# Causal attention in two score passes: first unit's stacked rows in sequence, value products in halves, and an earlier copy of the output's first half

## The chip, the cores and the metric

The kernel runs on one core of a Trainium2 chip. The metric is device time in microseconds: the time of one launch, in several runs, with their median. One further execution was profiled; every row below is of that one.

The engines have short names here, as in the profile: PE is TensorE's matmul side and PEld its weight loads, DVE is VectorE, ACT is ScalarE, POOL is GpSimd, SP is SyncE. SP and ACT each issue DMAs on a hardware queue of their own: q1 in the profile is SP's, q10 is ACT's.

## The reference, cut to what matters

The input is x with 2 sequences of 1024 tokens and 128 features. Four stages add to it one after the other: a causal attention at three sets of weights ("a"), six layers of local attention with a feed-forward part, a causal attention with linear biases ("b"), and the six layers again. The change touches the two causal stages only. What they compute, per sequence and set of weights, with 16 heads of 8 features:

```python
q, k, v = proj(Wq, bq), proj(Wk, bk), proj(Wv, bv)          # 16 heads, 8 features each
scores = einsum('bhqd,bhkd->bhqk', q, k) * scale            # causal: k <= q
m = max(scores, axis=-1)
e = exp(scores - m)
w = e / (sum(e, axis=-1) + 1e-06)
out = einsum('bhqk,bhkd->bhqd', w, v)
```

Stage "a" has six such units (two sequences by three weight sets), with an output projection and two layer norms behind them; stage "b" has two units with a bias per head and no norm.

## The kernel before, in words

All of a causal stage is in the function `causal` (from line 266). Each engine runs its own program, written out by hand, and all of them walk the same order: an outer loop over steps g (`STEPS`), an inner loop over 38 items n. Semaphores tie them together.

**Steps and items.** A unit's 16 heads are four quads of four heads; step g works on quad g % 4 of unit g // 4. Two score passes run at once. The first pass, of quad g, takes the scores with queries on partitions, item by item as in `FIRST` (38 items, each one bank of 512 columns, some of one matmul, some of two or four, eight of them on the diagonal with a mask matmul ahead); DVE reduces each item to its maxima (line 674). The second pass, of quad g - 2, takes the scores with keys on partitions and the negated maxima as three further rows of the contraction (`SECOND`, 36 items, eight with a mask); ACT takes the exponential of each (line 772). Stage "a" has 24 quads, "b" has 8. So a stage has two steps with the first pass alone, 22 or 6 with both, and two with the second alone, which are its tail.

**Stacked rows.** q and k are split into three bf16 parts, written to a scratch in DRAM (line 488, SP), and read back so that 48 partitions hold the six products of parts that are needed: lower heads on partitions 0 to 63, upper heads on 64 to 127. A set is six DMAs of 8 partitions by 16 KB. For the first unit of a stage SP issues q's rows, the lower in step -4 and the upper in step -2 (`stack`, line 504), and ACT issues k's rows, lower and then upper, in `stack_first_keys` (line 818) at step -3. For later units SP issues both. The lower rows are needed by quads 0 and 1 of a unit, the upper by quads 2 and 3: at line 545 PE waits, in steps 0 and 2 of a unit, for `stack_in[0]` or `stack_in[1]`. The two passes of one step lie on different halves of the partitions, so that they run side by side in PE.

**Banks.** The first pass has PSUM banks 0 to 2, the second 3 to 5, in turn. Before the scores of an item PE waits until the item three before it has been reduced (`s1_free`) or exponentiated (`s2_free`). Bank 6 holds the output of a quad, first half (512 queries), then second half. Bank 7 is for side matmuls (`beside`): projections, transposes, layer norms, one at most every third item, behind items with n % 3 == 1.

**Value products.** `GROUPS` cuts the 36 items of the second pass into ten groups of four or two items. When the last item of the group after it has been issued (n = 7, 9, 13, 17, 21, 25, 29, 33, 35, and 2 of the next step for the last), PE issues all value matmuls of a group in one go (`values`, line 579; matmuls at line 594): pieces of 128 to 512 columns, each from 128 keys to 32 output partitions, so that four heads run side by side on PE's columns. The first group has 16 pieces, the second 8, the third 4, the fourth 16, the next four 4 each, then 8 and 4. They are f32 and show as two records each. Exponentials lie in `pt`, which has room for three groups.

**Copies of the output.** The first half of a quad's output is complete after three groups, the second after ten. ACT copies each out of bank 6 (`take_out`, line 782): the first half behind the exponential of item 16, the second behind item 5 of the next step. Before the fourth group, at item 17, PE waits for the first copy (`ot_done`), and before the first group of the next quad, at item 7, for the second.

Of the kernel before, what the change touches and what calls it, by code (L numbers as in the profile page):

```python
# [86 lines left out]

FIRST = first_items()
SECOND, GROUPS = second_items()
GROUP_OF = [k for k, (lo, hi) in enumerate(GROUPS) for _ in range(lo, hi)]  # L90
PLAN = (("causal", "a"), ("layers", 0), ("causal", "b"), ("layers", 1))


def build(nc, t, out, scratch):
    with ExitStack() as ctx:
# [149 lines left out]
        at = [0]  # L245
# [20 lines left out]
        def causal(kind):  # L266
# [62 lines left out]
            with ExitStack() as local:  # L329
# [133 lines left out]
                with nc.Block() as block:  # L463
                    @block.sync
                    def _(sp):
                        def place_maxima(g):
                            if not 0 <= g < 4 * U:
                                return
                            G = 4 * u0 + g
                            rows, h0, par = rows_of(g, KS)  # L470
                            sp.wait_ge(m_step, 4 * G + 4)
                            if G:
                                sp.wait_ge(m_in, 48 * G)
                            for c in range(3):
                                r = rows.start + KF + c
                                sp.dma_start(qs[par][r:r + 1, h0:h0 + 4, :].rearrange("p h (q n) -> p (h q) n", n=P),
                                             mparts[0:4 * QT, c, :]).then_inc(m_in, 16)

                        def write_parts(u):
                            if not 0 <= u < U:  # L480
                                return
                            I = u0 + u
                            if I >= 2:
                                for h in range(2):
                                    sp.wait_ge(stack_in[h], 192 * (I - 1))
                            for a in range(2):
                                sp.wait_ge(split[3], 4 * I + 2 + 2 * a)
                                sp.dma_start(scratch[u % 2, a].rearrange("c p n -> p c n"), parts[:, a, :, :]).then_inc(part_out[a], 16)

                        def stack(u, h):  # L490
                            if not 0 <= u < U:
                                return
                            I = u0 + u
                            if u >= 2:
                                sp.wait_ge(s2_ready, 36 * (4 * (I - 2) + 2 * h + 2))
                            if I:
                                sp.wait_ge(stack_in[h], 192 * I)
                            for a, (combo, to) in enumerate(((COMBO_Q, qs[u % 2]), (COMBO_K, ks[u % 2]))):
                                if u == 0 and a == 1:
                                    continue  # L500
                                sp.wait_ge(part_out[a], 16 * (I + 1))
                                for n, c in enumerate(combo):
                                    r = 64 * h + 8 * n
                                    sp.dma_start(to[r:r + 8, :, :],
                                                 scratch[u % 2, a, c, 64 * h:64 * h + 64].rearrange("(h d) n -> d h n", d=HD)).then_inc(stack_in[h], 16)

                        def next_weights(u):
                            if not 2 <= u < U:
                                return
                            sp.wait_ge(side_free, order["value", u - 2, 1] + 1)  # L510
                            load_unit(sp, u)

                        def next_out_weights(u):
                            if not 1 <= u < U or kind == "b":
                                return
                            sp.wait_ge(side_free, order["join", u - 1, 1] + 1)
                            load_out(sp, u)

                        for g in STEPS:
                            i, q = divmod(g, 4)  # L520
                            place_maxima(g - 1)
                            if q == 0:
                                write_parts(i + 1)
                                stack(i + 1, 0)
                            elif q == 1:
                                next_out_weights(i - 1)
                            elif q == 2:
                                next_weights(i + 2)
                                stack(i + 1, 1)

                    @block.tensor
                    def _(pe):
# [43 lines left out]
                                    if x == len(second) - 1:  # L576
                                        ins.then_inc(s2_ready, 1)

                        def values(g, k):
                            if not 0 <= g < 4 * U:  # L580
                                return
                            G = 4 * u0 + g
                            c = 0 if k < 3 else 1
                            if k == 0:
                                pe.wait_ge(vq_ready, G + 1)
                                if G:
                                    pe.wait_ge(ot_done, 2 * G)
                            elif k == 3:
                                pe.wait_ge(ot_done, 2 * G + 1)
                            lo, hi = GROUPS[k]  # L590
                            pe.wait_ge(s2_free, len(SECOND) * G + hi)
                            pieces = [(b, piece) for b in range(lo, hi) for piece in SECOND[b]]
                            for b, (j, kt, q0, w, diag, at) in sorted(pieces, key=lambda one: (one[1][1], one[1][0])):
                                ins = nc.tensor.matmul(ps[32 * j:32 * j + 32, 6, q0 - c * CH:q0 - c * CH + w], vq[:, G % 2, kt, j, :],
                                                       pt[:, (len(GROUPS) * G + k) % 3, b - lo, at:at + w],
                                                       start=diag and kt % 4 == 0, stop=True, skip_group_check=True)
                            ins.then_inc(values_done, 1)

                        def beside(what, u, x):

# [50 lines left out]
                        for g in STEPS:  # L651
                            for n in range(len(FIRST)):
                                scores(g, n)
                                if n == 2:
                                    values(g - 3, len(GROUPS) - 1)
                                for k in range(len(GROUPS) - 1):
                                    if n == GROUPS[k + 1][1] - 1:
                                        values(g - 2, k)
                                if n % 3 == 1 and n < 36 and side_at(g, n // 3):
                                    beside(*side_at(g, n // 3))  # L660

# [100 lines left out]
                    def _(act):  # L762
# [48 lines left out]
                        def stack_first_keys():  # L811
                            act.wait_ge(part_out[1], 16 * (u0 + 1))
                            for h in range(2):
                                if u0:
                                    act.wait_ge(stack_in[h], 192 * u0)
                                for n, c in enumerate(COMBO_K):
                                    r = 64 * h + 8 * n
                                    act.dma_start(ks[0][r:r + 8, :, :],
                                                  scratch[0, 1, c, 64 * h:64 * h + 64].rearrange("(h d) n -> d h n", d=HD)).then_inc(stack_in[h], 16)

                        for g in STEPS:
                            if g == -3:
                                stack_first_keys()
                            for n in range(len(FIRST)):
                                if n < len(SECOND):
                                    exponentials(g - 2, n)
                                if n == 5:
                                    take_out(g - 3, 1)
                                elif n == 16:
                                    take_out(g - 2, 0)  # L830
                                if n % 3 == 2 and n < 37:
                                    before = side_at(g, n // 3 - 1) if n >= 3 else None
                                    if before and before[0] == "project":
                                        part(*before[1:], 1)
                                    if side_at(g, n // 3):
                                        beside(*side_at(g, n // 3))
# [957 lines left out]
```

## Time and profile before

| | |
|---|---|
| median of 3 runs | 5032.56 us (5029.35 to 5033.88) |
| the profiled execution's own time | 5031.75 us |
| its span, first to last instruction | 5030.0 us |
| PE busy | 4547.3 us, 90% |
| PEld busy | 2702.9 us, 54% |
| DVE busy | 3756.1 us, 75% |
| ACT busy | 3470.0 us, 69% |
| mean granted clock of TensorE | 0.940 |
| line 674, DVE's reductions of the first pass, stage "a" | 912 of 657 ns, 561.8 us |
| line 772, ACT's exponentials, stage "a" | 864 of 600 ns, 475.3 us |

The span is what lies between the first and the last instruction; the rest of the time is launch and end. Busy shares are means over four stages with different limits: here the first causal stage takes about the first fifth of the span, the second lies between 2844 and 3204 us, and the rest is the layers, which the change does not touch. A granted clock of 1.0 is 2.4 GHz, of 0.5 it is 1.2 GHz. A matmul's recorded end is modelled, so starts are safer to read than lengths: matmuls of one kind overlap in the records.

### The profile page before, as it was taken

What the parts mean: (1) busy time and instruction counts of PE and PEld (TensorE: products, weight loads), DVE (VectorE), ACT (ScalarE), POOL (GpSimd) and SP (SyncE); (2) the same over time, 40 slices, a digit from 0 to 9 for tenths busy, and PEclk for the clock granted to TensorE, in tenths of its full rate; (3) what the DMA queues carried; (4) which work ended last, traced back from release to release, by engine and by line L of the source; (5) the groups of instructions that cost most, each with busy time, mean ns of one, the idle gap of its engine ahead of it and who ended that gap; (6) DMA issues with size and microseconds to landing.
All of it is one profiled execution on the core that took longest, in us unless ns stands there. A gap on an engine that the chain in (4) does not pass through costs nothing. (4 is left out here: it accounts for less than half of the span.)

```text
span 5030.0 us, 122883 instructions
## 1 busy us (share of the span) xinstructions
PE 4547.3 (90%) x49788; PEld 2702.9 (54%) x49788; DVE 3756.1 (75%) x5802; ACT 3470.0 (69%) x5475; POOL 2201.6 (44%) x1271
## 2 busy tenths in 40 slices
PE   5998989869999999999999599789999999999997
PEld 2333433336666666666666233256666666666664
DVE  4777777257888888888887277278888888888884
ACT  1666666437878887887877136368888787888884
POOL 1111010036656565665654010066566565656561
PEclk6999999779999999999999679789999999999998
DMA  3211220000000000000000120000000000000000
GB/s 80 42 38 28 37 41 3 2 32 10 10 6 19 2 24 2 15 10 15 10 6 2 43 46 2 32 10 10 2 15 10 15 10 15 10 2 24 2 6 9
DMA packets 70035, 87.77 MB, mean 17 GB/s; under 512 B 22532, under 2 KB 44288, under 8 KB 68864
## 3 DMA queue, kind: packets, MB, share of 16 engines
q1 hardware_dynamic: 67720, 76.41, 6.5%
q8 instruction: 416, 6.82, 0.6%
q10 hardware_dynamic: 1728, 3.15, 0.4%
q14 instruction: 171, 1.40, 0.1%
HBM read 65.11 MB, written 13.63 MB: 16 GB/s over the span
## 5 line engine op out<-in xcount | busy, mean ns | idle before, releaser
L1078 PE MATMUL ps<-l_wqk,l_xa 128*128 128x512 f32 x1536 | 772.7, 627 | 42.8 <-DVE l_rs L1544 42.8
L674 DVE TENSOR_REDUCE a_pm<-ps 128x1 f32<-128x512 f32 (+3 forms) x912 | 561.8, 657 | 213.1 <-PE ps L568 208.1
L1188 PE MATMUL ps<-l_yb,l_mh 128*128 128x256 f32 x3072 | 710.1, 381 | 2.5 <-issue 2.5
L772 ACT ACTIVATE a_pt<-ps 128x512 f32<-128x512 f32 x864 | 475.3, 600 | 334.1 <-PE ps L574 331.9
L1501 POOL TENSOR_TENSOR l_pn<-l_pe,l_rl 128x1024 f32<-128x1024 f32 x192 | 365.2, 1902 | 558.6 <-DVE l_rl L1582 558.5
L1188 PEld LDWEIGHTS ps<-l_yb,l_mh 128*128 128x128 f32 x3072 | 564.3, 190 | 74.7 <-issue 5.6
L1544 DVE TENSOR_TENSOR l_rs<-ps,l_tab 128x512 f32<-128x512 f32 x768 | 491.1, 681 | 0.0
L1078 PEld LDWEIGHTS ps<-l_wqk,l_xa 128*128 128x128 f32 x1536 | 276.4, 194 | 379.4 <-issue 298.4
L1492 POOL TENSOR_TENSOR l_qkn<-l_rc,l_rn 128x1024 f32<-128x1024 f32 x192 | 386.4, 2013 | 202.5 <-DVE l_rn L1562 202.5
L1484 POOL TENSOR_TENSOR l_rc<-l_rc,l_rs 128x1024 f32<-128x1024 f32 x192 | 452.0, 2354 | 44.3 <-DVE l_rs L1544 44.3
L1552 DVE TENSOR_REDUCE l_ss<-l_sq 128x16 f32<-128x1024 f32 x384 | 464.9, 1211 | 2.8
L1172 PE MATMUL ps<-l_ptl,l_xw 64*128 64x256 f32 x3072 | 444.2, 407 | 19.6 <-DVE l_yb L1592 13.4
L1331 ACT ACTIVATE l_sq<-ps 128x1024 f32<-128x1024 f32 x384 | 388.9, 1013 | 89.0 <-PE ps L1078 87.5
L1254 PE MATMUL ps<-l_lnx,l_w 128*128 128x512 f32 (+1 forms) x576 | 319.1, 637 | 113.7 <-ACT l_gl L1444 101.0
L1402 ACT ACTIVATE l_yb<-ps 128x256 f32<-128x256 f32 x768 | 251.2, 380 | 220.9 <-PE ps L1172 220.7
L1172 PEld LDWEIGHTS ps<-l_ptl,l_xw 64*128 64x128 f32 x3072 | 270.0, 188 | 240.8 <-issue 136.0
L1484 POOL TENSOR_TENSOR lnc<-lnc,l_rs 128x1024 f32<-128x1024 f32 x96 | 226.0, 2354 | 335.2 <-DVE l_rs L1544 335.2
L568 PE MATMUL ps<-a_ks,a_qs 48*128 48x128 bf16 (+3 forms) x1728 | 319.2, 290 | 58.4 <-DMA a_ks<-scratch 38.4
L1592 DVE COPY l_yb<-ps 128x256 f32<-128x256 f32 x768 | 288.2, 417 | 60.7 <-PE ps L1172 40.7
L1484 POOL TENSOR_TENSOR lnq<-lnq,l_rs 128x1024 f32<-128x1024 f32 x96 | 226.3, 2357 | 240.0 <-DVE l_rs L1544 240.0
L1366 ACT ACTIVATE l_kt<-ps 128x512 f32<-128x512 f32 x384 | 207.8, 594 | 177.9 <-PE ps L1084 177.9
L574 PE MATMUL ps<-a_qs,a_ks 51*128 51x128 bf16 (+3 forms) x1728 | 307.9, 286 | 0.9 <-ACT a_pt L772 0.7
(225 smaller groups left out, 9054.3 us busy)
## 6 DMA issues: line engine op xcount, KB each, us to landing
l_wqk<-in_lWqkv SPq DMA_DIRECT2D x24, 512.0 KB, 4.5
scratch<-a_parts SPq DMA_DIRECT2D x12, 768.0 KB, 4.2
a_qs<-scratch SPq DMA_DIRECT2D x72, 128.0 KB
a_ks<-scratch SPq DMA_DIRECT2D x60, 128.0 KB
l_wvt<-in_lWvT SPq DMA_DIRECT2D x12, 512.0 KB, 4.9
l_wo<-in_lWo SPq DMA_DIRECT2D x12, 512.0 KB, 6.6
l_w<-in_lW SPq DMA_DIRECT2D x12, 341.0 KB, 2.8
scratch<-b_parts SPq DMA_DIRECT2D x4, 768.0 KB, 4.7
```

The lines of the kernel that those rows point to most:

```text
L568: ins = nc.tensor.matmul(ps[:, bank1, at1:at1 + w], qs[par][rows, h0 + j, qt * P:(qt + 1) * P], ks[par][rows, h0 + j, k0:k0 + w], start=no ...
L674: nc.vector.tensor_reduce(to, src, AX.X, ALU.max).then_inc(s1_free, 1)
L772: nc.scalar.activation(pt[:, K % 3, n - GROUPS[k][0], :], ps[:, 3 + N2 % 3, :], ACT.Exp).then_inc(s2_free, 1)
L1078: last = nc.tensor.matmul(ps[:, x, :], xa[:, u, o:o + P], wqk[:, a * INNER + x * CH:a * INNER + (x + 1) * CH], start=True, stop=True)
L1172: last = nc.tensor.matmul(ps[:, 4 + e, w * 256:(w + 1) * 256], xw[rows, t % 2, ww, :], ptl[rows, :, 32 * ww:32 * ww + 32], start=w == 0, s ...
L1188: last = nc.tensor.matmul(ps[:, 6, 0:2 * P], mh[:, h, :], yb[:, n % 2, h, :], start=h == 0, stop=h == LH - 1, skip_group_check=True)
L1331: nc.scalar.activation(sq[:, a, :].rearrange("p (x n) -> p x n", x=2), ps[:, 0:2, :], ACT.Square).then_inc(N["qk"[a] + "_squared"], 1)
L1484: nc.gpsimd.tensor_tensor(turned(t, a), turned(t, a), rs[:, a, :], ALU.add).then_inc(N["qk"[a] + "_rotated"], 1)
L1492: nc.gpsimd.tensor_tensor(qkn[:, a, :].rearrange("p (h d) -> p h d", d=LD), turned(t, a).rearrange("p (h d) -> p h d", d=LD), rn[:, a, :]. ...
L1501: nc.gpsimd.tensor_tensor(pn[:, :, :], pe_[:, :, :], rl[:].unsqueeze(2).to_broadcast([P, LH, 2 * WIN]), ALU.mult).then_inc(N["p_done"], 1)
L1544: ins = nc.vector.tensor_tensor(dsin[:, :, lo:lo + 32], src[:, :, hi:hi + 32], tab[:, 2 * a + 1, t % QT, lo:lo + 32].unsqueeze(1).to_broad ...
L1552: nc.vector.tensor_reduce(ss[:, a, :], sq[:, a, :].rearrange("p (h d) -> p h d", d=LD), AX.X, ALU.add).then_inc(N["qk"[a] + "_summed"], 1)
```

## The change

Three edits, in the functions of the causal stages. First, for the first unit of a stage the upper stacked rows are issued only when the lower ones, of q and of k, have landed: SP waits for `stack_in[0]` in `stack`, ACT in `stack_first_keys`. Second, a group's value matmuls are issued in two halves: the first where the whole group was, the second one item later (for the last group at items 1 and 2 in place of 2). Groups of more than four pieces are cut by pieces; groups of four pieces have each piece cut in two by columns, which makes eight. Third, ACT copies the first half of the output behind item 14 in place of 16.

```diff
--- before.py
+++ after.py
@@ -87,6 +87,21 @@
 
 FIRST = first_items()
 SECOND, GROUPS = second_items()
+
+
+def half_groups():
+
+    out = []
+    for lo, hi in GROUPS:
+        pieces = sorted(((b, piece) for b in range(lo, hi) for piece in SECOND[b]), key=lambda one: (one[1][1], one[1][0]))
+        if len(pieces) > 4:
+            out.append((pieces[:len(pieces) // 2], pieces[len(pieces) // 2:]))
+        else:
+            out.append(tuple([(b, (j, kt, q0 + h * w // 2, w // 2, diag, at + h * w // 2)) for b, (j, kt, q0, w, diag, at) in pieces] for h in range(2)))
+    return out
+
+
+HALVES = half_groups()
 GROUP_OF = [k for k, (lo, hi) in enumerate(GROUPS) for _ in range(lo, hi)]
 PLAN = (("causal", "a"), ("layers", 0), ("causal", "b"), ("layers", 1))
 
@@ -495,6 +510,8 @@
                                 sp.wait_ge(s2_ready, 36 * (4 * (I - 2) + 2 * h + 2))
                             if I:
                                 sp.wait_ge(stack_in[h], 192 * I)
+                            if u == 0 and h == 1:
+                                sp.wait_ge(stack_in[0], 192 * (u0 + 1))
                             for a, (combo, to) in enumerate(((COMBO_Q, qs[u % 2]), (COMBO_K, ks[u % 2]))):
                                 if u == 0 and a == 1:
                                     continue
@@ -576,25 +593,25 @@
                                     if x == len(second) - 1:
                                         ins.then_inc(s2_ready, 1)
 
-                        def values(g, k):
+                        def values(g, k, part):
                             if not 0 <= g < 4 * U:
                                 return
                             G = 4 * u0 + g
                             c = 0 if k < 3 else 1
-                            if k == 0:
+                            if part == 0 and k == 0:
                                 pe.wait_ge(vq_ready, G + 1)
                                 if G:
                                     pe.wait_ge(ot_done, 2 * G)
-                            elif k == 3:
+                            elif part == 0 and k == 3:
                                 pe.wait_ge(ot_done, 2 * G + 1)
                             lo, hi = GROUPS[k]
                             pe.wait_ge(s2_free, len(SECOND) * G + hi)
-                            pieces = [(b, piece) for b in range(lo, hi) for piece in SECOND[b]]
-                            for b, (j, kt, q0, w, diag, at) in sorted(pieces, key=lambda one: (one[1][1], one[1][0])):
+                            for b, (j, kt, q0, w, diag, at) in HALVES[k][part]:
                                 ins = nc.tensor.matmul(ps[32 * j:32 * j + 32, 6, q0 - c * CH:q0 - c * CH + w], vq[:, G % 2, kt, j, :],
                                                        pt[:, (len(GROUPS) * G + k) % 3, b - lo, at:at + w],
                                                        start=diag and kt % 4 == 0, stop=True, skip_group_check=True)
-                            ins.then_inc(values_done, 1)
+                            if part == 1:
+                                ins.then_inc(values_done, 1)
 
                         def beside(what, u, x):
 
@@ -651,11 +668,11 @@
                         for g in STEPS:
                             for n in range(len(FIRST)):
                                 scores(g, n)
-                                if n == 2:
-                                    values(g - 3, len(GROUPS) - 1)
+                                if n in (1, 2):
+                                    values(g - 3, len(GROUPS) - 1, n - 1)
                                 for k in range(len(GROUPS) - 1):
-                                    if n == GROUPS[k + 1][1] - 1:
-                                        values(g - 2, k)
+                                    if n in (GROUPS[k + 1][1] - 1, GROUPS[k + 1][1]):
+                                        values(g - 2, k, n - GROUPS[k + 1][1] + 1)
                                 if n % 3 == 1 and n < 36 and side_at(g, n // 3):
                                     beside(*side_at(g, n // 3))
 
@@ -813,6 +830,8 @@
                             for h in range(2):
                                 if u0:
                                     act.wait_ge(stack_in[h], 192 * u0)
+                                if h:
+                                    act.wait_ge(stack_in[0], 192 * (u0 + 1))
                                 for n, c in enumerate(COMBO_K):
                                     r = 64 * h + 8 * n
                                     act.dma_start(ks[0][r:r + 8, :, :],
@@ -826,7 +845,7 @@
                                     exponentials(g - 2, n)
                                 if n == 5:
                                     take_out(g - 3, 1)
-                                elif n == 16:
+                                elif n == 14:
                                     take_out(g - 2, 0)
                                 if n % 3 == 2 and n < 37:
                                     before = side_at(g, n // 3 - 1) if n >= 3 else None
```

## Rows read from the trace of the kernel before

**Rows 1.** Windows by stage, first causal stage: start, steady part, tail.

```profile
core 0: us, PE busy (x) PEld busy (x) DVE busy (x) ACT busy (x) POOL busy (x), PEclk, DMA share, GB/s
26.00:70.70 44.70, 3.80 (x7) 0.89 (x6) 3.00 (x4) 4.70 (x8) 9.09 (x8) 0.60 0.42 92
...
276.00:884.00 608.00, 549.32 (x5557) 236.21 (x5553) 468.22 (x869) 383.90 (x699) 57.10 (x109) 0.96 0.15 29
...
909.00:981.20 72.20, 68.05 (x456) 21.99 (x454) 1.91 (x4) 40.05 (x77) 1.73 (x5) 0.65 0.02 3
```

**Rows 2.** Timelines of SP, ACT, PE at both stages' starts: start, length, [idle <- releaser].

```profile
40.47 5.20 SPq L504 DMA_DIRECT2D a_qs<-scratch  x12
...
89.05 8.49 SPq L488 DMA_DIRECT2D scratch<-a_parts  x2
...
44.92 12.79 ACTq L818 DMA_DIRECT2D a_ks<-scratch  x12
81.29 0.63 ACT L791 ACTIVATE a_parts<-a_qkf 128x512 bf16<-128x512 f32 x1 [42.50 <-DVE a_qkf L705]
...
70.75 1.46 PE L568 MATMUL ps<-a_ks,a_qs 48*128 48x512 bf16 x3 [38.40 <-DMA a_ks<-scratch]
...
2894.14 1.46 PE L568 MATMUL ps<-b_ks,b_qs 54*128 54x512 bf16 x3 [35.26 <-DMA b_ks<-scratch]
```

**Rows 3.** DMA queues (packets, MB, share) in 45:53, 54.5:68.5 (both), 71:77 us.

```profile
q1 hardware_dynamic: 314, 0.57, 52.9%
...
q10 hardware_dynamic: 408, 0.75, 27.3%
q1 hardware_dynamic: 396, 0.72, 25.8%
...
q10 hardware_dynamic: 258, 0.48, 52.4%
```

**Rows 4.** Waits from 131 to 981 us: total us, times, longest.

```profile
DVE a_pm L674 <- PE ps L568: 159.3, 228, 3.4
PEld ps L568 <- DVE a_pm L674: 133.3, 234, 2.0
...
PEld ps L594 <- issue: 61.4, 218, 1.7
...
PEld ps L594 <- ACT a_ot L782: 25.6, 24, 4.3
```

**Rows 5.** Waits from 2955 to 3204 us (second causal stage).

```profile
PEld ps L594 <- ACT b_ot L782: 9.3, 8, 1.4
```

**Rows 6.** Timelines of ACT and PE around one copy, 447.5 to 454.5 us.

```profile
450.92 0.60 ACT L782 ACTIVATE a_ot<-ps 128x512 f32<-128x512 f32 x1
...
451.57 1.88 PE L594 MATMUL ps<-a_pt,a_vq 128*32 128x128 f32 x32 [0.67 <-ACT a_ot L782]
```

**Rows 7.** Timeline of PE, 417 to 422 us: scores, values, mask.

```profile
417.82 0.39 PE L568 MATMUL ps<-a_ks,a_qs 48*128 48x512 bf16 x1
...
418.05 0.38 PE L568 MATMUL ps<-a_ks,a_qs 48*128 48x512 bf16 x1
...
418.36 1.06 PE L594 MATMUL ps<-a_pt,a_vq 128*32 128x512 f32 x8
419.35 0.39 PE L550 MATMUL ps<-a_mask_q,identb 128*128 128x512 bf16 x1
```

**Rows 8.** Timelines of PE and DVE around one burst, 403 to 409 us.

```profile
404.76 1.08 PE L594 MATMUL ps<-a_pt,a_vq 128*32 128x128 f32 x32 [0.46 <-issue]
...
407.05 0.69 DVE L674 TENSOR_REDUCE a_pm<-ps 128x4 f32<-128x512 f32 x1 [1.22 <-PE ps L568]
```

**Rows 9.** Timelines of PE and ACT in the tail, 966 to 975 us.

```profile
968.24 1.93 PE L594 MATMUL ps<-a_pt,a_vq 128*32 128x512 f32 x8
970.10 1.96 PE L574 MATMUL ps<-a_qs,a_ks 51*128 51x512 bf16 x4
...
970.80 2.06 ACT L772 ACTIVATE a_pt<-ps 128x512 f32<-128x512 f32 x4 [1.69 <-PE ps L574]
```

## The prediction

> **What bounds the kernel now.** I read the stretches by stage first [rows 1]. The two causal stages are the only ones touched. The first has a start with TensorE (PE) all but idle (26 to 70.7 us), a steady part, and a tail after the last reduction (909 to 981 us) in which only the second score pass is left. In the steady part no engine is full: PE is recorded busy 549 of 608 us (its ends are modelled), VectorE (DVE) 468, ScalarE (ACT) 384. So I went to the waits.
>
> In the start, PE's first score matmul waits 38.4 us for stacked rows of k [rows 2]; the second stage has the same wait, 35.3 us. In the steady part two engines are late in turn [rows 4]: DVE waits 159.3 us for PE's scores, and PE's loads wait 133.3 us for DVE to free a bank. That is the mark of a load that comes in bursts with three banks of cover, not of one full engine. One burst: 32 value matmuls start at 404.76 after an idle 0.46, and DVE's next reduction comes 1.22 us late [rows 8]. And at the fourth group PE waits for ACT's copy of the output's first half: 25.6 us in 24 waits in the first stage [rows 4], 9.3 in 8 in the second [rows 5], so 34.9 us in 32. The example shows why: the copy runs at 450.92, behind the exponential of item 16, and the values follow at 451.57 [rows 6].
>
> **Part 1: upper stacked rows behind the lower.** SP issues twelve copies of q from 40.47, ACT twelve of k from 44.92, six of each lower [rows 2]. Each is 128 KB, 0.131 MB. From 45 to 53 us only SP's queue moves, 0.57 MB in 8 us, 71 GB/s: q lower. From 54.5 to 68.5 the two queues share, 0.75 and 0.72 MB in 14 us: k lower runs beside q upper, at half of 105 GB/s. Alone (71 to 77 us) ACT's queue moves 0.48 MB in 6 us, 80 GB/s [rows 3].
> With q upper held back, k lower has its stretch to itself: it begins near 54 and takes 0.786 MB / 76 GB/s (between 71 and 80) = 10.3 us, to 64.3; about 0.7 for the landing makes 65.0 in place of 70.75. I take 5.6 us a stage, **11 us** for two. Lower end: 71 GB/s gives 11.1 us and 4.9 a stage. Upper end: 10 a stage (rival E). Steps 0 and 1 behind it move as a whole, since their wait for these rows ends last.
>
> What stands behind the new waits: SP's next issue is at 89.05 and ACT's next instruction at 81.29 after 42.5 us of idleness [rows 2], both led by PE's first step, so near 83 and 75.5 afterwards; waits that end at 65, with six issues each behind them, are over by then. Upper rows: twelve copies, 1.57 MB at 105 GB/s, 15 us, landed near 82. They are needed at step 2, two steps of 38 reductions of 0.69 us [rows 8] after the start, so not before 115. Cost nothing; without that cover it would be up to 15 us.
>
> **Part 2a: the copy of the output's first half behind item 14.** The three groups it copies are then issued in full directly after item 14's scores, and ACT copies before it does items 15 and 16. PE's wait before the fourth group should go: 28 of the 32 waits lie in steps with both passes, 28 x 1.09 = **30.5 us**; the four in the tails are 4.4. Lower bound: ACT's copy (0.60, [rows 6]) now delays exponentials 15 and 16, and PE meets that at item 18 as a wait for a bank; then half is left. I take it whole: item 18 is late behind exactly this wait, and PE is the late engine there. The wait of 0.46 before the first group [rows 8], for the copy of the second half behind item 5, is not touched.
>
> **Part 2b: halves.** Columns streamed stay the same. Added per step are 24 matmuls with their loads (six groups of four pieces become eight); four pieces run side by side on 32 columns each, so I cost the issue at nothing, the streams of the neighbours hiding it. If nothing hid them, six more sets of four would cost at most what a change of tiling costs (0.10 us, below) each, 0.6 us a step.
> What costs is the change of tiling. Scores of 512 columns start 0.23 us apart (417.82, 418.05), the values start 0.31 after the last score; eight value records start at 418.36 and the mask at 419.35, 0.99 us, of which some 0.87 is streaming [rows 7]. So a change costs about 0.10 us. A second half brings two changes where scores follow it (items 8, 14, 18, 30) and one where a mask or a side matmul follows (2, 10, 22, 26, 34, 36): 14 changes, 1.4 us a step, 39 us over 28 steps. It lands on the path where PE is the late engine. PE waits about as long for DVE as DVE for PE [rows 4], so I take half, **20 us lost**; ends 0 and 39. At the other end, the table's idle gap of 61.4 us / 218 = 0.28 us before a value group [rows 4] bounds the price of a whole second visit.
> The Trainium skill ("TensorEngine Tiling (Array Packing)", Key Properties) says that changing the tiling mode drains TensorE, which speaks against halving; its page "TensorE: Matmul & The Clock Gate" (Single matmul latency) puts a drain near 175 ns. By that, as an estimate, 14 x 0.175 x 28 / 2 = 34 us are lost and the sum is 14 us higher; the rows show 0.10, and I keep that.
>
> The gain of halving: a burst of 0.87 us ahead of the next score shrinks by up to 0.44, so DVE's late item comes earlier [rows 8], but the other half follows one item later. Where PE stays late through the next items (after groups 0 to 2, and 7 to 9) nothing is won; where it has slack again, up to 0.44 is. Ends 0 and 4 such bursts x 0.44 x 28 = 49 us. I take 0.2 us a step, **6 us**, near the lower end, as the copy's wait already held the largest of these stalls.
>
> **Tails** (four steps in two stages). PE is at the lower clock level for much of it (granted clock 0.65 over the tail, [rows 1]) and is the bound: scores, values, scores follow at 968.24 and 970.10 without a wait while ACT idles 1.69 us [rows 9]. Some 18 changes a step (fewer masks and sides) at 0.15 us, between the 0.10 at the upper clock and 0.2 at half speed, are 2.7 x 4 = 10.8 us; less the 4.4 us of waits that go, **6.4 us lost**.
>
> **Sum.** -11 - 30.5 + 20 - 6 + 6.4 = -21 us. The profiled execution took 5031.75 us (span 5030.0 and 1.75 around it), 0.8 below the median of the three runs, 5032.56. 5031.75 - 21 = **5011 us**.
>
> **Rivals.**
> A, slower: the second visits decide. PE is late throughout, and each second half costs it the 0.28 us of [rows 4], in the tail some 0.35 (between 0.28 and its double at half speed): 28 x 10 x 0.28 + 4 x 10 x 0.35 = 92 us against 11 + 35 of gains: +46, 5078. It decides from 46 / 320 = 0.144 us a visit. For it: PE's recorded share [rows 1]. Against: PE's waits for DVE, as long as DVE's for it.
> B, halving works: DVE's waits behind bursts shrink by a further 0.1 us at each of ten groups, 28 us: 4983; at 0.15 us, 42 us, 4969. For: the 159.3 us that DVE waits [rows 4]. Against: the second half follows one item later.
> C, the steady part nets to nothing, the wait for the copy coming back as one for a bank: -11 + 6.4, 5027.
> D, the start gains nothing, because k lower alone goes no faster than it did shared: -10, 5022. Against: 80 GB/s alone to 53 shared [rows 3].
> E, both lower sets share from 45 us at 105 GB/s: 1.57 MB in 15 us, landed near 60.7, 10 a stage in place of 5.6: 5002. Against: ACT's queue moved nothing before 53 though it had issued [rows 3]. The Trainium skill ("DMA: Bandwidth & Descriptors", Queues, rings and completion order) has each DMA engine go round its queue rows packet by packet, which would give E; the trace agrees from 54.5 us on, not before.
>
> **How the numbers follow.** Forecast 0.38, A 0.08, B 0.24, C 0.18, D 0.04, E 0.08. 0.2% is 10 us, about what a measurement of this kernel can tell from no change. Faster by more: nearly all of the forecast, B, E, half of D, some of C: 0.76. Within: most of C, half of D and an edge of the forecast: 0.16. Slower: A, 0.08. The range goes from B's 4969 to 5037, which is C with 10 us more of mode changes; outside are A and the far end of B.
>
> **What would show it.** The first scores of the two stages at about 65 and 2888.5 instead of 70.75 and 2894.14, with ACT's queue full-rate from 54 us and the upper rows landed by 85. No wait of value matmuls for the copy but the one at item 7. Twice the value groups at half the length, each with its 0.1 us on both sides; DVE's waits for PE lower in total, more in number. Tail steps about 1.5 us longer. The forecast is wrong if the steps between reductions' ends grow (A), if they stay while the wait only changes its name (C), or if they shrink by over 1.5 us each (B).

## The result, and the profile after

The changed kernel took 5002.97 us (median of 4 runs, 4992.34 to 5010.29) against 5030.95 for the kernel before on the same chip: a ratio of 0.9947 [0.9934, 0.996], 28 us faster. Forecast were 5011, and 21 us. The execution that was profiled is the slowest of the four (5010.29 us, span 5008.5, 1.78 around it); its span is 21.5 us under the one before, so a sum made on its rows falls 6.5 us short of the medians.

The sum came out; its terms did not. This table splits the spans at the first score reduction of a stage, at the ends of the steps (DVE's gather reductions) and at ACT's last copy. Us, profiled executions:

| stretch | before | after | difference | forecast |
|---|---|---|---|---|
| start to first reduction, first stage | 71.4 | 66.2 | -5.2 | -5.6 |
| steps 0 and 1, both stages | 120.5 | 120.6 | +0.1 | 0 |
| steps 2 to 23, first stage | 777.3 | 780.9 | +3.6 | } |
| steps 2 to 7, second stage | 183.1 | 179.8 | -3.3 | } -16.5 (-30.5 + 20 - 6) |
| tail, first stage | 72.2 | 65.5 | -6.7 | } |
| tail, second stage | 65.7 | 63.3 | -2.4 | } +6.4 |
| layers and second start | 1913.6 | 1907.0 | -6.6 | -5.6 |
| layers at the end | 1826.2 | 1825.2 | -1.0 | 0 |

**The start** did what was forecast. First the timelines of SP, ACT and PE in the changed kernel (start, length, what, and in brackets the idle time before it with its releaser), to be held against [rows 2]:

```profile
40.95 26.91 SPq L521 DMA_DIRECT2D a_qs<-scratch  x12
...
83.90 8.49 SPq L503 DMA_DIRECT2D scratch<-a_parts  x2
...
45.42 22.88 ACTq L837 DMA_DIRECT2D a_ks<-scratch  x12
76.14 0.63 ACT L808 ACTIVATE a_parts<-a_qkf 128x512 bf16<-128x512 f32 x1 [36.87 <-DVE a_qkf L722]
...
65.59 1.46 PE L585 MATMUL ps<-a_ks,a_qs 48*128 48x512 bf16 x3 [32.77 <-DMA a_ks<-scratch]
...
2879.29 1.46 PE L585 MATMUL ps<-b_ks,b_qs 54*128 54x512 bf16 x3 [32.22 <-DMA b_ks<-scratch]
```

From SP's first issue to the first scores are 65.59 - 40.95 = 24.6 us, where they were 70.75 - 40.47 = 30.3. The issuing of twelve copies is stretched from 5.20 to 26.91 on SP and from 12.79 to 22.88 on ACT: that is the new wait. Nothing useful stood behind it, since SP's next issue and ACT's next instruction came at 83.90 and 76.14, each some 5 us sooner than before. The DMA queues of the changed kernel (packets, MB, share), in 45:53 and then in 56:63:

```profile
q1 hardware_dynamic: 322, 0.58, 53.6%
q10 hardware_dynamic: 1, 0.00, 0.2%
...
q10 hardware_dynamic: 316, 0.58, 52.1%
q1 hardware_dynamic: 1, 0.00, 0.0%
```

ACT's queue (q10) has the second stretch to itself, at 0.58 MB / 7 us = 83 GB/s where it shared in [rows 3].

**The steady part** as a whole did not move, though its waits did. Waits of the changed kernel from 126 to 973 us (total, times, longest), with [rows 4] as the counterpart:

```profile
DVE a_pm L691 <- PE ps L585: 160.2, 277, 2.6
PEld ps L585 <- issue: 132.0, 415, 1.3
PEld ps L585 <- DVE a_pm L691: 91.8, 193, 2.0
...
PEld ps L610 <- ACT a_ot L799: 3.3, 9, 0.8
```

The wait for ACT's copy, 25.6 us in 24, has shrunk to 3.3 us in 9 (last row). DVE waits for PE as long as before (159.3), only more often, 277 times in place of 228. So PE hands its scores over no sooner: what was taken off one wait was added elsewhere.

**The tail** is the place where the forecast had the wrong sign. Windows of the changed kernel (columns as in [rows 1]): the first tail, and the two parts of it:

```profile
907.40:973.00 65.60, 63.78 (x562) 22.57 (x562) 1.93 (x5) 41.17 (x77) 1.74 (x5) 0.74 0.02 4
907.40:938.40 31.00, 29.60 (x316) 11.57 (x315) 1.93 (x5) 23.68 (x45) 1.74 (x5) 1.00 0.03 7
938.40:972.50 34.10, 33.68 (x240) 10.71 (x244) 0.00 (x0) 17.40 (x32) 0.00 (x0) 0.50 0.00 0
```

The granted clock over the tail rose from 0.65 to 0.74. Its halves show that this is no middle level: the full 2.4 GHz for 31.0 us, then 1.2 GHz for 34.1. PE is recorded busy nearly all through both, so the tail's length goes with the clock.

### The profile page after: what moved, and what is told of

It reads as the page before. It is cut to its first block and busy times, and to the rows that moved or that the text cites. A ratio compares the mean times of both kernels' runs of the same rounds, so it can differ in the third digit from the quotient of the medians.

```text
span 5008.5 us, 125957 instructions
## 1 busy us (share of the span) xinstructions
PE 4584.8 (92%) x51324; PEld 2718.1 (54%) x51324; DVE 3760.3 (75%) x5802; ACT 3480.4 (69%) x5475; POOL 2201.4 (44%) x1271
## 5 line engine op out<-in xcount | busy, mean ns | idle before, releaser
L585 PE MATMUL ps<-a_ks,a_qs 48*128 48x128 bf16 (+3 forms) x1728 | 332.4, 291 | 44.1 <-DMA a_ks<-scratch 32.8
L591 PE MATMUL ps<-a_qs,a_ks 51*128 51x128 bf16 (+3 forms) x1728 | 318.8, 285 | 0.5 <-ACT a_pt L789 0.3
```

The source lines that it names most:

```text
L585: ins = nc.tensor.matmul(ps[:, bank1, at1:at1 + w], qs[par][rows, h0 + j, qt * P:(qt + 1) * P], ks[par][rows, h0 + j, k0:k0 + w], start=no ...
```

## The experiments

All ten compute the full result. Ratios are to the kernel before on the same chip, with a 95% interval; a gain or loss in us is worked out from the ratio unless medians are named. First each part alone, and the changed kernel once more beside them.

**Start only**

```diff
+                            if u == 0 and h == 1:
+                                sp.wait_ge(stack_in[0], 192 * (u0 + 1))
...
+                                if h:
+                                    act.wait_ge(stack_in[0], 192 * (u0 + 1))
```

> Only the order of the first unit's stacked rows. Theory (forecast's term): the first scores of each stage come 4.4 to 5.6 us earlier, as in the trace of the changed kernel, and nothing else moves: 10 us less in all, near 5021. Rival: what is won at the start is lost behind it, as the steps behind are paced by something else: within 3 us of before.

5018.17 us (12 runs), 0.9985 [0.9975, 0.9995]: 7.5 us faster, between 2.5 and 12.5. The first scores in its timeline:

```profile
64.95 1.46 PE L585 MATMUL ps<-a_ks,a_qs 48*128 48x512 bf16 x3 [32.44 <-DMA a_ks<-scratch]
...
2879.51 1.46 PE L585 MATMUL ps<-b_ks,b_qs 54*128 54x512 bf16 x3 [29.83 <-DMA b_ks<-scratch]
```

The steps and the tails behind them stay as long as before (775.3 and 182.9; 71.2 and 67.1). The term stands, and nothing behind it gives it back.

**Copy only**

```diff
-                                elif n == 16:
+                                elif n == 14:
```

> Only the copy of the output's first half behind item 14. Theory: PE's wait before the fourth group goes (34.9 us in the trace of before) and the steps with both passes shorten by about 0.8 us each: 25 to 35 us less, near 5001. Rival: the wait comes back as a wait for a bank at item 18, since ACT now copies before exponentials 15 and 16: at most 10 us less.

4978.74 us (5 runs), 0.9904 [0.9888, 0.9919]: 48 us faster, more than the whole change. Only 17.6 of it lie in the steps (777.3 to 764.8, 183.1 to 178.0); the tails went from 72.2 and 65.7 to 52.1 and 53.3. Its waits from 126 to 896 us:

```profile
DVE a_pm L689 <- PE ps L583: 146.7, 233, 5.1
PEld ps L583 <- DVE a_pm L689: 137.3, 237, 2.0
...
PEld ps L565 <- DVE a_pm L689: 48.7, 74, 3.0
...
PEld ps L609 <- ACT a_ot L797: 2.5, 8, 0.4
```

and those of the kernel before over the same steps, 126 to 909 us:

```profile
DVE a_pm L674 <- PE ps L568: 159.6, 229, 3.4
PEld ps L568 <- DVE a_pm L674: 134.5, 236, 2.0
...
PEld ps L550 <- DVE a_pm L674: 42.2, 64, 3.0
...
PEld ps L594 <- ACT a_ot L782: 22.9, 22, 4.3
```

The wait for the copy goes from 22.9 us to 2.5, and 2.8 + 6.5 = 9.3 us come back as PE waiting for DVE to free a bank, ahead of scores and masks. The remainder, 11.1, is near the 12.5 us by which these 22 steps got shorter: when PE no longer waits for ACT it runs into DVE.

**Halves only**

```diff
-                                if n == 2:
-                                    values(g - 3, len(GROUPS) - 1)
+                                if n in (1, 2):
+                                    values(g - 3, len(GROUPS) - 1, n - 1)
...
-                                    if n == GROUPS[k + 1][1] - 1:
-                                        values(g - 2, k)
+                                    if n in (GROUPS[k + 1][1] - 1, GROUPS[k + 1][1]):
+                                        values(g - 2, k, n - GROUPS[k + 1][1] + 1)
```

> Only the halves, the copy still behind item 16. Theory: changes of tiling cost more than shorter bursts give, most of all in the steps with eight transposes (third quad of a unit, 1.2 us longer in the trace of the changed kernel): 5 to 25 us more, near 5045. Rival: the halves are what won: 15 us less or better, near 5015, the copy's wait shrinking too because the fourth group starts with half.

5064.58 us (5 runs), 1.0084 [1.0069, 1.01]: 42 us slower (37 by the medians). The steps grew by 17.2 and 2.2 us, the tails by 1.8 and 4.8. Waits from 126 to 985 us:

```profile
DVE a_pm L689 <- PE ps L583: 174.9, 290, 2.6
...
PEld ps L608 <- ACT a_ot L797: 27.0, 24, 4.3
```

DVE waits longer for PE, not less, and the wait for the copy stays.

**The whole change again**, unedited.

> The changed kernel again, all three parts. Near 5003, spread over some 15 us. If the parts add, its gain is the sum of the three alone; if the halves only pay once the copy is out of the way, it is more.

4992.62 us (6 runs, 4986.55 to 5005.96), 0.9942 [0.9926, 0.9959]. The profiled execution (span 4986.0) is 22.5 us shorter than the one of the section above. The steps are the same, 781.4 and 179.9; the tails are 55.5 and 50.8 in place of 65.5 and 63.3, which is 22.5 us. The whole difference between two executions of one kernel lies in its tails: 10.2 us of the first were at the lower clock here, 34.1 there. The three parts alone add up to 13.5 us by their ratios, the whole has 29; the halves alone have the longest tails (74.0 and 70.5), but the record doesn't settle where all of that difference lies.

Next, what in the halves costs: the added matmuls, or going back to them a second time?

**Start and copy, no halves**: the changed kernel with `values` and its loop as they were.

> Start order and copy behind item 14, values in one go as before. If the parts add (start alone -8 to -10 us, copy alone -49, halves alone +37): 4970, some 22 us below all three together. If the halves cost only while the copy is late, it is level with all three together, near 4993.

4966.74 us (4 runs), 0.9876 [0.9861, 0.9891]: against the whole change 26 us less by the medians and 33 by the ratios.

**All three, both halves issued in one go**: the same matmuls, one visit to a group.

```diff
-                                if n in (1, 2):
-                                    values(g - 3, len(GROUPS) - 1, n - 1)
+                                if n == 2:
+                                    for part in range(2):
+                                        values(g - 3, len(GROUPS) - 1, part)
...
-                                    if n in (GROUPS[k + 1][1] - 1, GROUPS[k + 1][1]):
-                                        values(g - 2, k, n - GROUPS[k + 1][1] + 1)
+                                    if n == GROUPS[k + 1][1] - 1:
+                                        for part in range(2):
+                                            values(g - 2, k, part)
```

> All three parts, but both halves of a group issued in one go where the group was: the 24 more matmuls a step are there, the second visit and its changes of tiling are not. Theory (changes of tiling are the price): within 5 us of the kernel with start and copy and no halves, near 4972, steps of the third quad back at 33.7 us. Rival (the added matmuls and loads are the price): as the changed kernel or slower, near 4993 to 5000, those steps at 34.9 us.

4965.59 us (4 runs), 0.9874 [0.9859, 0.9889]: level with no halves. So the added matmuls cost nothing, and the price is that of the second visit. It is seen best in a step of the third quad, whose length hardly varies. DVE's gather reductions at the two ends of such a step, in the kernel before,

```profile
399.90 0.25 DVE L681 TENSOR_REDUCE a_nm<-a_pm 128x32 f32<-128x96 f32 x1
...
433.60 0.25 DVE L681 TENSOR_REDUCE a_nm<-a_pm 128x32 f32<-128x96 f32 x1
```

in the changed kernel,

```profile
390.85 0.25 DVE L698 TENSOR_REDUCE a_nm<-a_pm 128x32 f32<-128x96 f32 x1
...
425.78 0.25 DVE L698 TENSOR_REDUCE a_nm<-a_pm 128x32 f32<-128x96 f32 x1
```

and with both halves in one go:

```profile
387.04 0.25 DVE L700 TENSOR_REDUCE a_nm<-a_pm 128x32 f32<-128x96 f32 x1
...
420.74 0.25 DVE L700 TENSOR_REDUCE a_nm<-a_pm 128x32 f32<-128x96 f32 x1
```

33.70, 34.93 and 33.70 us: 1.2 us for the second visits. By the means of five steps each (4 to 23), the changed kernel's steps are 0.9 us longer than those of the kernel without halves in the first and the fourth quad, and 0.3 shorter in the second. That quad's steps are no good scale: they differ by 1.0 between the two kernels without second visits (33.24 and 32.27). The waits from 126 to 907 us, both halves in one go:

```profile
DVE a_pm L693 <- PE ps L585: 143.5, 232, 2.1
PEld ps L585 <- issue: 103.6, 334, 0.9
PEld ps L585 <- DVE a_pm L693: 103.4, 223, 1.6
```

Against these the changed kernel has 132.0 / 415 on the line "issue": 81 more idle moments before scores, 28 us more, with no releaser that the profile can name; its waits for DVE ahead of scores are 11.6 us less.

Then the tail by itself.

**Copy behind item 14 in the tail steps alone**, on the kernel before.

```diff
-                                elif n == 16:
+                                elif n == (14 if g >= 4 * U else 16):
```

> The kernel before, with the copy behind item 14 only in the two last steps of a stage, where the first pass is done. Theory (in the tail PE's wait for the copy is what lets TensorE's clock fall to its lower level): tails of 52 and 53 us with the clock up, steps 2 to 23 as before: 30 us less, near 4997. Rival (the tail's clock is kept by what the steps before it do): tails as before, 72 and 66 us, at most 5 us less.

4991.32 us (5 runs), 0.9926 [0.9912, 0.994]: 37 us faster by an edit that touches four steps. The kernel before, windows of the first tail and, as the last line, the second tail whole:

```profile
909.00:922.70 13.70, 12.46 (x119) 5.23 (x116) 1.91 (x4) 9.17 (x18) 1.73 (x5) 1.00 0.07 13
922.70:943.20 20.50, 19.44 (x100) 5.06 (x104) 0.00 (x0) 10.67 (x21) 0.00 (x0) 0.50 0.00 1
943.20:950.00 6.80, 5.81 (x81) 2.88 (x71) 0.00 (x0) 4.83 (x9) 0.00 (x0) 1.00 0.00 0
950.00:980.70 30.70, 29.84 (x160) 8.67 (x162) 0.00 (x0) 15.38 (x29) 0.00 (x0) 0.50 0.00 1
3138.00:3204.00 66.00, 61.49 (x456) 19.91 (x455) 0.54 (x3) 40.64 (x77) 1.74 (x5) 0.72 0.01 1
```

What PE and ACT did at the first fall, in the timelines of the kernel before (the stop begins at 922.51, the recorded end of the matmul ahead of it):

```profile
922.92 0.62 ACT L782 ACTIVATE a_ot<-ps 128x512 f32<-128x512 f32 x1
...
923.59 1.93 PE L594 MATMUL ps<-a_pt,a_vq 128*32 128x128 f32 x32 [1.08 <-ACT a_ot L782]
```

With the copy moved in the tails, their two windows, the same value matmuls, and the copy's wait over the steps before (126 to 912 us):

```profile
912.70:964.80 52.10, 46.77 (x455) 17.85 (x453) 1.87 (x4) 39.97 (x77) 1.74 (x5) 1.00 0.02 4
3121.10:3171.30 50.20, 45.16 (x453) 17.47 (x453) 0.50 (x2) 40.36 (x77) 1.74 (x5) 1.00 0.01 2
...
926.23 1.08 PE L594 MATMUL ps<-a_pt,a_vq 128*32 128x128 f32 x32
...
PEld ps L594 <- ACT a_ot L782: 22.9, 22, 4.3
```

With the copy earlier that idle microsecond is gone, the clock stays at 1.00 through both tails and the same 32 records take 1.08 instead of 1.93 us. The four waits of about 1.1 us that go in the tails are worth 35.6 us there, since the lower clock went with them. The fall is recorded 0.2 us into the stop, so the trace by itself does not show that the stop brought it; the run does, as only the copy's place is changed. The steps keep their wait, 22.9 in 22.

**Both halves in one go in the tail steps alone**, the rest of the change as it is.

> All three parts, but in the two last steps of a stage both halves are issued in one go. Theory (second visits cost some 0.9 us a step with both passes, and in the tail they let the clock fall again in some executions): tails of 52 us with the clock up as without halves, the steps with both passes as in the changed kernel; about 10 us below all three parts together, near 4983, and some 17 above the kernel without halves. Rival (the tail of the changed kernel is short of clock for another reason): tails of 55 to 65 us, level with all three parts.

4989.88 us (5 runs), 0.9929 [0.9915, 0.9942]. Its tails are 54.0 and 53.4, level with the whole change's second execution. The ratio overlaps with that of the whole change, so this doesn't settle whether it is the second visits that let the clock fall in some executions of the changed kernel.

Last, two versions that follow from the readings.

**Start, copy, no halves, and the second half's copy behind item 3** in place of 5 (`n == 3` for `take_out(g - 3, 1)`).

> Start and copy behind 14, no halves, and the copy of the output's second half behind item 3 in place of 5. Theory: PE's idle 0.46 us before the first group of a quad goes in 30 steps: 8 to 14 us below the kernel with start and copy alone, near 4960. Rival: PE is bounded by DVE there, level with it.

4962.4 us (4 runs), 0.9866 [0.985, 0.9882]: 4 under the version without it, inside the intervals, so the 8 to 14 that were expected are not shown. Its tails (51.6 and 49.7) and its clock there, 1.00 in both, are like those of the next version.

**The same with the first copy behind item 13** (`n == 13` and `n == 3`).

> Start, no halves, copies behind items 13 and 3. Theory: with groups issued in one go the first half is complete behind item 13, but PE has no wait for it left to lose: level with copies behind 14 and 3, near 4962. Rival: an earlier copy delays fewer exponentials ahead of item 18: up to 10 us less.

4952.55 us (4 runs, 4951.77 to 4954.38), 0.9851 [0.9836, 0.9866]. The fastest of all by its median, though its interval overlaps with that of the version before it: 74 us under the kernel before, and 40 under the whole change's second set of runs. Steps 757.3 and 177.2, tails 51.6 and 49.7.

## Why the prediction was right, and where it was not

**Start: right.** 5.6 us a stage were forecast; 24.6 against 30.3 in the first and 25.4 against 29.8 in the second make 5.6 and 4.4, together 10.0 for 11. Rival D (nothing gained) falls by the runs of the start alone, rival E by the queues: ACT's moved one packet before 53 us, as in [rows 3]. The Trainium skill ("DMA: Bandwidth & Descriptors", Queues, rings and completion order) has each DMA engine go round the queue rows that it has work for; the trace shows no such turns before 53 us, and no run shows whether ACT's queue had work there yet. One number inside the step was off: the upper rows, forecast for 82, were moving until about 89. The cover (115) held.

**Copy in the steady part: right in kind, 12 us too large.** The failed step is "I take it whole". Steps 2 to 23 of the first stage last 777.3, 775.3 and 781.3 us where the code in them is that of before (before, start only, tail only), and 764.8, 767.4 and 762.0 with the copy moved and no second visits: by the means 13.2 less. With 5.1 in the second stage, where each three agree to 0.2, that is 18.3 for 30.5. The bound from below, that half would return as a wait for a bank, was the nearer one. Of the 20.4 us that went, 9.3 returned in the one profile of the copy alone, so rival C's mechanism is real, at nearly half.

**Halves: right in kind, 4 us too small.** Forecast were 20 lost and 6 won, net +14. The runs give the net alone. The three profiled executions with all edits in the steps have 780.9, 781.4 and 780.8 us, by the mean 16.3 over the three without second visits, and 1.7 in the second stage: 18.0. That is 18.0 / 28 = 0.64 us a step, where the prediction had half of 1.4 less 0.2, 0.5. How it arises shows in PE's timeline of the changed kernel (the second pass's scores, which run beside, are left out):

```profile
383.52 0.64 PE L610 MATMUL ps<-a_pt,a_vq 128*32 128x256 f32 x8
384.09 0.33 PE L585 MATMUL ps<-a_ks,a_qs 48*128 48x384 bf16 x1
...
384.41 0.64 PE L610 MATMUL ps<-a_pt,a_vq 128*32 128x256 f32 x8
384.99 0.33 PE L585 MATMUL ps<-a_ks,a_qs 48*128 48x384 bf16 x1
...
385.31 0.39 PE L567 MATMUL ps<-a_mask_q,identb 128*128 128x512 bf16 x1
```

A half takes 0.57 us from its start to the scores' start (0.58 the other). Two are 1.15, where the eight records of full width took 0.99 in [rows 7]: 0.16 us more. The way into the second half is not in this: it starts 0.32 us after the scores (384.09 to 384.41), where scores start 0.23 apart in [rows 7]. So a second visit costs PE some 0.16 to 0.25 us, as an estimate, ten of them 1.6 to 2.5 us a step, of which 0.64 reach the end. The Trainium skill ("TensorEngine Tiling (Array Packing)", Key Properties) says that a change of tiling mode drains the engine. The runs agree, since the same matmuls in one visit cost nothing, though they don't single out the drain from the rest of a second visit. By the 175 ns that the prediction takes from its page "TensorE: Matmul & The Clock Gate" (Single matmul latency) the net would have been +28, as an estimate; the price from the rows was the nearer one. Rival A needed 0.144 us a visit on the path to make the change slower; it is 18.0 / 280 = 0.064. Rival B falls, and the gain of 6 us is not to be seen either: DVE's waits for PE are 160.2 us with the halves and 143.5 with the same matmuls in one visit, so the shorter burst brings no score earlier on the whole.

So copy and halves, 18.3 won and 18.0 lost, cancel in the steady part: the changed kernel's steps are as long as before.

**Tails: wrong sign.** "6.4 us lost" is the step that failed. I took the lower clock of [rows 1] as given, priced four waits at their own 1.1 us, and added tiling changes. But the clock falls at such a wait. The kernel before shows 1.00 up to 922.7 and 0.50 after it, with PE idle from 922.51 to 923.59. With the copy moved in the tails, and nothing else, that idle time is gone, the tails run at 1.00 and they are 35.6 us shorter. The Trainium skill ("TensorE: Matmul & The Clock Gate", A second HAM failure mode: psum-queue depth-cycling) describes a kernel whose short idle moments between groups of matmuls made the clock swing; the trace agrees in kind, with stops of 1.08 us here. With the tail's windows around the fall read beforehand, a term of the other sign would have been among the rivals.

The changed kernel takes only part of that gain: 9.1 us in its first profiled execution, 31.6 in the second. Its timelines of PE and ACT before the fall at 938.4 have two short stops of PE:

```profile
937.31 0.88 PE L591 MATMUL ps<-a_qs,a_ks 51*128 51x384 bf16 x4 [0.25 <-ACT a_pt L789]
...
938.11 0.62 ACT L799 ACTIVATE a_ot<-ps 128x512 f32<-128x512 f32 x1
...
938.82 1.08 PE L610 MATMUL ps<-a_pt,a_vq 128*32 128x128 f32 x16 [0.64 <-issue]
```

Both are shorter than the first copy's was. The longer ends as ACT's copy of the output's second half does, the one behind item 5, which the change left alone. The kernel before has this stop too, and the second fall in its first tail, at 950.0, comes 1.2 us behind it:

```profile
948.13 0.62 ACT L782 ACTIVATE a_ot<-ps 128x512 f32<-128x512 f32 x1
...
948.85 1.08 PE L594 MATMUL ps<-a_pt,a_vq 128*32 128x128 f32 x32 [0.64 <-issue]
```

The other three falls in its tails (922.7, 3151.6, 3185.8) lie at the copy that the change moves. So the low clock that is left in the changed kernel begins at a second wait, not at a remainder of the first. That wait doesn't always bring a fall: the kernel with the copy moved in the tails alone keeps it,

```profile
944.29 1.08 PE L594 MATMUL ps<-a_pt,a_vq 128*32 128x128 f32 x32 [0.64 <-issue]
```

and stays at 1.00. In the second tails of the copy alone, of no halves and of both halves in one go, the clock falls there as well, but is back after 3.4 us, against 34.1 us in each tail of the changed kernel's first execution and 6.8 and 3.4 in its second. That the second visits make the difference is argued, not shown: versions with the copy early in every step and without second visits have tails of 49.7 to 53.3 in every profile, but the run made to single it out was inconclusive. What decides whether the clock falls at the second wait, and how long it stays down, is open.

**The sum** was right by luck, because errors met: start 1 short, copy 12 short, halves 4 worse, which is 17 less gain than forecast, against tails 15 to 38 better. It pointed the wrong way on what to keep: the halves, priced as nearly paid for by the rest, are the part to drop.

## What to carry to other kernels

Look at the granted clock inside a lightly loaded stretch, not its mean: where it falls at a stop of TensorE, take the stop away and measure, since the slower matmuls after it can cost more than the stop, here 35.6 us for 4.4. A wait between two engines that are late in turn is worth less than its rows where, as here, the next wait is already there (18.3 us for 30.5). Where TensorE changes tiling for small groups, don't go back to a group twice to shorten its burst; move the consumer's copy earlier instead.

## What the runs showed of the hardware

In a tail in which TensorE was recorded busy 12.46 of 13.70 us, its clock went from 2.4 to 1.2 GHz at a stop of 1.08 us and stayed there for 20.5 us, though it was recorded busy 19.44 of them. With the copy moved there was no such stop and no fall, in both tails. A stop of 0.64 us at another place was followed by a fall in some tails and not in others.

In the steady part the clock falls too, for at most 13.7 us at a time once step 2 is under way. All in all, steps 2 to 23 have 60 us at 1.2 GHz in the kernel before, 64 in the changed one and 58 with the copy alone. By the means over the three profiles of each kind they have 58, 63 and 61 us (code of before, all edits, copy moved without second visits), so the gain and the loss in the steps are not the clock's. The scatter within a kind may be in part: start only, with 47 us, has the shortest steps of its kind, and tail only, with 68, the longest.

And a DMA queue that had issued was slow to begin beside another: ACT's moved nothing and then one packet in 45 to 53 us, before and after the change, while SP's moved 314 and 322, though ACT had issued from 44.92 and 45.42. Whether the other queue holds it back or its start takes that long by itself, no run shows.
